# Stores merged into one step and a load on its own semaphore, in the closing of layer zero and the merge of layer one of a four-layer graph stack

## The reference, cut to what matters

```
h = relu(layernorm(x));  x = x + L0(h)     # 3 attention passes, batch-normed inputs, summed
h = relu(layernorm(x));  x = x + L1(h)     # graph attention + a Mamba scan, gated, MLP, layernorm
h = relu(layernorm(x));  x = x + L2(h)     # weighted neighbour sums, two 256x256 products
h = relu(layernorm(x));  x = x + L3(h)     # neighbour sums, two 256x256 products
```

## Time and profile before

| | us |
|---|---|
| median of 3 runs | 7790.14 |
| lowest, highest | 7788.18, 7800.23 |
| the profiled execution | 7791.36 |
| its span in the trace | 7789.4 |

### The profile page before, as it was taken

How to read it: one execution, slowest core, us unless ns; L and a number is a source line. 1 busy time by engine, 2 the same in 40 slices (tenths; PEclk the granted TensorE clock), 3 DMA queues, 4 the chain that set the end, 5 groups by cost and what they waited for, 6 DMA issues and landing times. The chain is left out here.

```text
span 7789.4 us, 93332 instructions
## 1 busy us (share of the span) xinstructions
PE 5313.0 (68%) x20089; PEld 3414.3 (44%) x20089; DVE 5065.8 (65%) x10805; ACT 3288.2 (42%) x11052; POOL 4469.2 (57%) x4306
## 2 busy tenths in 40 slices
PE   4656688888888545657777774775666665656555
PEld 4623344444444333224444442654444443444444
DVE  7677588888888753569999994664555553333333
ACT  1124466666666423778988894441000000000000
POOL 2150166666666253057777773324777775777775
PEclk9978899999999756779999996997888787888887
DMA  5114488888888663379998996223555556555556
GB/s 197 22 63 110 156 274 278 276 285 278 276 279 280 197 207 117 112 250 321 321 321 316 322 308 167 76 68 107 177 178 180 176 181 126 170 170 165 170 171 134
DMA packets 544576, 1554.19 MB, mean 200 GB/s; under 512 B 135295, under 2 KB 245899, under 8 KB 528650
## 3 DMA queue, kind: packets, MB, share of 16 engines
q0 software_dynamic: 234976, 829.97, 36.1%
q1 hardware_dynamic: 280348, 694.68, 25.2%
q10 hardware_dynamic: 28844, 25.07, 1.0%
HBM read 1183.69 MB, written 593.47 MB: 228 GB/s over the span
## 5 line engine op out<-in xcount | busy, mean ns | idle before, releaser
L1263 POOL DMA_INDIRECT rows_e<-hidden,unit_src x1856 | 1765.5, 951 | 628.5 <-issue 542.9
L618 POOL DMA_INDIRECT rows_e<-table,unit_src x928 | 1071.3, 1154 | 803.9 <-PE acc_e L823 385.8
L1000 POOL DMA_INDIRECT rows_e<-table,unit_src x928 | 1069.1, 1152 | 373.8 <-issue 269.0
L1291 DVE SCALAR_TENSOR_TENSOR sums_e<-sums_e,unit_keep,acc_e 128x256 f32<-128x256 f32 x928 | 444.1, 479 | 1212.1 <-PE acc_e L1372 1209.6
L1372 PE MATMUL acc_e<-rows_e,same 128*128 128x256 f32 x1856 | 707.1, 543 | 666.5 <-DMA rows_e<-hidden,unit_src 651.1
L812 ACT ACTIVATE rows_e<-rows_e 128x64 f32<-128x64 f32 x4640 | 1119.1, 333 | 1.9
L1084 ACT ACTIVATE rows_e<-rows_e 128x64 f32<-128x64 f32 x3712 | 919.9, 333 | 3.8
L1372 PEld LDWEIGHTS acc_e<-rows_e,same 128*128 128x128 f32 x1856 | 487.7, 278 | 845.9 <-DMA rows_e<-hidden,unit_src 708.5
L1416 ACT ACTIVATE turned_f<-turn_f 128x512 f32<-128x512 f32 x98 | 58.5, 597 | 1882.3 <-PE turn_f L1388 1882.3
L823 PE MATMUL acc_e<-rows_e,unit_w 128*128 128x512 f32 (+1 forms) x1856 | 704.9, 526 | 144.7 <-DVE rows_e L805 101.0
L1372 PE MATMUL acc_e<-rows_e,links 128*128 128x256 f32 x1856 | 514.3, 425 | 324.5 <-DMA rows_e<-hidden,unit_src 324.1
(11 more groups left out here) (467 smaller groups left out, 9548.2 us busy)
## 6 DMA issues: line engine op xcount, KB each, us to landing
bc<-bc_rows SPq DMA_DIRECT2D x228, 896.0 KB, 6.6
summed<-sums_e SPq DMA_DIRECT2D x464, 390.0 KB
staged<-sums_e SPq DMA_DIRECT2D x116, 1024.0 KB, 4.5
summed<-sums_e SPq DMA_DIRECT2D x464, 130.5 KB
rows_e<-table,unit_src POOLq DMA_INDIRECT x1856, 5.6
hots<-hot_e SPq DMA_DIRECT2D x116, 256.0 KB, 5.0
hots<-unit_w SPq DMA_DIRECT2D x116, 256.0 KB, 4.9
rows_e<-hidden,unit_src POOLq DMA_INDIRECT x1856, 2.8
```

The costliest lines, as they stand in the source:

```text
L618: pool.indirect_dma_start(self.rows[:, v, e, :], None, table, bass.IndirectOffsetOnAxis(unit_src[:, u, e:e + 1], 0)).then_inc(self.landed[ ...
L1000: pool.indirect_dma_start(self.rows[:, v, e, :], None, self.tab, bass.IndirectOffsetOnAxis(unit_src[:, u, e:e + 1], 0)).then_inc(self.land ...
L1263: pool.indirect_dma_start(self.rows[:, v, e, :], None, tab, bass.IndirectOffsetOnAxis(unit_src[:, u, e:e + 1], 0)).then_inc(self.landed[v ...
L1291: dve.scalar_tensor_tensor(self.sums[:, at_, :], self.sums[:, (n - 1) % self.SUMS, :], unit_keep[:, u:u + 1], self.acc[:, n % self.ACCS, 0 ...
```

## The change

In the closing, the store of x (step 15) and the two empty turns behind it go; x and the normalised rows are stored in one `move` after the layer norm, x first. A job has 31 steps in place of 34.

In the merge, the load of x is no longer a step of the lane. ACT waits for what the lane has issued, issues the load, and a semaphore of the lane's own (`x_in`) counts it. The second product of the MLP follows in the same turn and does not wait for it; DVE waits for `x_in` just before x is added. The store of x moves into the last step, ahead of that of the normalised rows. A job has 61 steps in place of 63, and the next job begins 64 turns after this one in place of 66.

```diff
@@ close_and_project
                     yield ch.step(dve, lambda: dve.tensor_tensor(x3, x3, part[0], ALU.add))
-                    yield ch.move(lambda e: e.dma_start(blk(x_dram), x3))
-                    yield
-                    yield
                     yield from layer_norm(ch, x3, t3, stat[:, k, :, :], relu=True)
-                    yield ch.move(lambda e: e.dma_start(blk(h_dram), t3))
+                    yield ch.move(lambda e: e.dma_start(blk(x_dram), x3), lambda e: e.dma_start(blk(h_dram), t3))
                     yield ch.scatter(pool, *[lambda b=b: pool.indirect_dma_start(
@@ ahead of merge
             chain.wait(act)
+            x_in, drawn_x = [sem(f"x_in{k}") for k in range(LANES)], [0] * LANES
@@ merge
                     yield ch.step(act, lambda: act.activation(fT[j], ff, ACT.Relu, bias=fb[:, j:j + 1]))
-                yield ch.move(lambda e: e.dma_start(a3, blk(x_dram)))
+                ch.wait(act)
+                act.dma_start(a3, blk(x_dram)).then_inc(x_in[k], 16)
+                drawn_x[k] += 16
                 yield ch.step(pe, *[f for b in range(m) for f in
...
                 yield from layer_norm(ch, l3, l3, st, gain=vecs["ln2_g"][:, :], shift=vecs["ln2_b"][:, :])
+                dve.wait_ge(x_in[k], drawn_x[k])
                 yield ch.step(dve, lambda: dve.tensor_tensor(a3, a3, l3, ALU.add))
-                yield ch.move(lambda e: e.dma_start(blk(merged_x[:, :]), a3))
                 yield from layer_norm(ch, a3, l3, st, relu=True)
-                yield ch.move(lambda e: e.dma_start(blk(hidden[0][0:NP, :]), l3))
+                yield ch.move(lambda e: e.dma_start(blk(merged_x[:, :]), a3), lambda e: e.dma_start(blk(hidden[0][0:NP, :]), l3))
```

## The result

| | before, us | after, us |
|---|---|---|
| median of 4 runs each | 7789.16 | 7717.72 |
| lowest to highest | 7786.20 to 7800.23 | 7716.84 to 7728.71 |
| profiled execution | 7791.36 | 7728.71 |

The ratio is 0.9909, 95% interval 0.9892 to 0.9926: 71 us faster at the medians, 63 between the two profiled executions, where 56 were forecast.

The account below looks back on a forecast made before the run. The prediction took the closing as bound by a chain of waits (POOL's scatter ladder) and the merge by PE near its limit plus its waits; -6 and -50 us gave -56, 7734 from the median of the runs, range 7685 to 7775.

Parts of the forecast that it names:

- The wait at L2551: Merge: PE's wait for the load of x, 43.3 us or 1.73 us per job, goes entirely.
- The clock: Merge: matmuls of L2551 run slow after a wait; half of that excess goes, 0.6 us per job.
- The exchange of waits: Merge: L2551 moves ahead on PE, waits for its relu instead of the blend; an exchange of equals, 0 us.
- the next wait takes the place: Rival, 0.15: in the merge L2551 waits for the relu behind other lanes' L493; merge gives 12 us, closing nothing, 7778.
- ACT's issue: Merge: ACT issuing a DMA per job, ahead of other lanes' L493, costs 0.3 us per job.
- The slower rival: Rival, 0.07: ACT is held by its DMA issue in the merge, 4.02 us each; +36 us, 7826.
- The x store of the merge: Merge: DVE's 16.4 us of waiting for the x store's landing lies beside PE's work; counted as nothing.
- The turns of the closing: Closing: three of 37 turns go from each job, 12 turns in all; 32 us less at best.
- The pair of stores: Closing: x store issued right before the h store delays the waiting scatter by issue and transfer share; 26 us more.
- rule of ring order: Closing: each DMA engine consumes a queue's descriptors in order, so h's bytes start after x's; 20 us more, whole 7754.
- Deeper: Rival, 0.20: PE closes up almost to its work in the merge, closing's turns come cheap; -100 us, 7690.
- The closing loses: Rival, 0.08: the closing's scatter waits for two stores amid the loads, +27 there, -50 in the merge; 7767.

Follow-up runs that it names:

- e3: Against the kernel before: in the merge only the load of x issued by ACT on its own semaphore, x store still its own step; merge 492.3 us, ratio 0.9947.
- e7: Changed merge, but the lane's carrier (SP or POOL) issues the load of x instead of ACT; closing as before; merge 486.0 us, whole 7785.53.
- e9: Against the kernel before: merge's x store joined with the last store, a bare turn kept in its place, load as before; merge 537.9 us, whole 7813.95.
- e2: Against the kernel before: the change's edits to the merge alone, closing as before; merge 485.8 us, ratio 0.9934.
- e4: Against the kernel before: in the merge only the stores joined in the last step, load of x still awaited, 65 turns; merge 520.6 us, ratio 0.9975.
- e8: Changed merge with two bare turns added at the end, so 66 turns between jobs; closing as before; merge 485.6 us, whole 7784.19.
- e6: Changed closing with its three turns gone, but x stored at its old place, awaited only by the lane's next load; merge unedited; closing 369.7 us.
- e10: The change, but the closing's x store back at its old place, awaited only by the lane's next load; closing 364.8 us, whole 7719.27, ratio 0.9893.
- e12: The change itself, repeated against the kernel before on the third chip; closing 380.1 us, merge 485.7, whole 7729.88, ratio 0.9916.
- e1: Against the kernel before: the change's edits to the closing alone, merge as before; closing 379.5 us, ratio 0.9979.
- e11: As e10, and in the closing the lane awaits neither the store nor the scatter of h, only its next load does; closing 302.1 us, ratio 0.9801.
- e5: Changed closing with stores joined but three bare turns kept before the layer norm; merge as before; closing 400.3 us, merge 543.3.

## Why the prediction was right

**The likeliest case happened, with its mechanism.** PE's waits were the price of the merge and POOL's ladder that of the closing. The merge was forecast at -50 and measured -56.5, the closing -6 and -12.0. The round of the merge was forecast at 119 and is 120.1.

**The wait at L2551 (-43.3):** gone, as said, in the change and also in e3 and e7, where only the load is taken out of the lane's waits or another engine issues it. That L2551 stands a turn earlier on PE is part of the same step, and its share is open. DVE's add of x waits for no DMA.

**The clock (-15):** PE's busy time in the merge fell by 19 us for the same instructions. The mean of L2551 was forecast near 400 ns and is 422 and 410, against 454 and 441 and a median of 379: somewhat less than half of the excess went there.

**The exchange of waits (0):** 22.1 us for the relu came and 27.4 of the 43.1 for the blend went (PE's wait, which the prediction in one place calls DVE's), -5. The wait for the relu is 0.9 us per job in the mean and 1.5 at most, as was forecast. So half of the old wait came back under another name, but the blend's paid for it: *the next wait takes the place*, at 12 us for the merge, did not happen.

**ACT's issue (+7.5):** nothing, by e7. Its issues took 0.37 us. The slower rival falls with it.

**The x store of the merge (0):** about 5 us by e9 in the kernel with the old load, within the noise; 6.5 on top of the new one by e2 and e3, where a turn goes with it. Beside it the prediction left out that a turn can matter: it could, 17 us in e4, as long as PE waited for the load, and did not afterwards (e8).

**PE's own times** close the sum: L2551 waits 43.3 - 22.1 = 21.2 us less, the first MLP product 27.4 less, the busy time is 19.1 less, and other waits grew by 13.6 (L513 for L493 from 42.0 to 51.0, those for ACT's transposes and relus by 4.6). That is -54.1 of the -56.5. The prediction had no term for waits that grow. That its total of -50 came near is in part luck: those 13.6 us stand against 7.5 that ACT's issue did not cost, 5.3 that the exchange gave and 4.1 that the clock gave beyond its term.

**The turns of the closing (-32):** -27.4 by e6 against e7 and e8, -30.8 by e10 against e9's unedited closing. **The pair of stores (+26):** +15.3 by e10 and e12, 0.6 us per job in place of 1.04. Both terms had the right sign and were too large, the pair more so, and as they have opposite signs the sum hid it. Of the pair's 1.04 us, 0.5 were a share of the transfer. On one chip the store of h lands 2.3 us after its issue in e10 and 2.6 behind the x store in e12 when SP issues it, 5.2 and 4.5 when POOL does: +0.3 and -0.7, where 0.5 had been added for both. The issues by themselves, 14 x 0.36 + 11 x 0.77 = 13.5 us, come near the whole price; this is an estimate, as no run has the one without the other. The step that failed is the expectation built on this term: POOL's wait in front of the scatter was to rise to about 120 us, and it fell to 81.2. The pair did lengthen it (74.1 to 85.9), but the prediction did not see that three turns fewer would shorten the same wait by 22 us (96.3 to 74.1). "POOL waiting less than before" was listed as a sign of being wrong; it was not one. The round of the closing was to be 98 us and is 92.9.

By the rule of ring order that the prediction took from the Trainium skill, "DMA: Bandwidth & Descriptors", section "Queues, rings and completion order", it had the closing at +14 and the whole at 7754. The same section says that a later descriptor may finish its write before an earlier one, so the full 1.3 us per job was the prediction's reading and not the page's. Measured is a price of 15.3 us for the pair in place of the 46 that these 1.3 us made, with the issue. The landing times bear on it: on SP the x store lands 2.3 us after its issue and the h store, issued 0.4 us later, 2.6 after its own, so h lands 0.7 us behind x. That is less than the 1.3 us at the round's rate. But the 204 GB/s of the round were moved by DMA engines that were busy for 0.62 of it; at full share that would be 329 GB/s and 0.8 us for 256 KB, an estimate with which the rule could still hold. It is neither shown wrong nor needed.

*Deeper* was the direction: the result is 7718, nearer to the forecast than to 7690. *The closing loses* is out by e1.

## What to carry to other kernels

In a pipeline of lanes that share engines in order, a wait costs what stands behind it on the engine; ask of each awaited DMA who reads or overwrites what it touches next, and put the wait there. A wait that got shorter in a trace doesn't prove that an edit was free: two parts of one change can move the same row in opposite directions, and only a kernel with one of them tells. e11 took waits out of the closing that no data needed, and gained 81 us on top of the 67 of the change on that chip.

## What the runs showed of the hardware

The kernel before took 7797 us on one chip and 8237 on another (medians); its granted clock was 0.857 to 0.863 on the first of these and 0.819 to 0.823 on the second. The unedited closing took 390.0 to 397.2 us on all of them, the unedited merge 542.6 to 549.6. The other stretches differ: from the end of the closing to the start of the merge it was 1768 us in the kernel before and 1861 in e1 on the slower chip, and behind the merge 2432 and 2751. What slows that chip was not looked into.

e6's merge, which has no edit, took 549.6 us where e5's took 543.3 on the same chip. Most of the 6 us is PE's busy time, 370.2 us against 364.8 for the same 1584 instructions, at a granted clock of 0.84 against 0.85; its waits are the same within 1 us each. Why the clock was lower no run shows, and differences of that size in a single run are not built on.
